# Moving the routing steps inside one attention turn of a fused encoder, attention and expert kernel

## The chip, the cores and the metric

One core of a Trainium2 chip runs the whole program in one launch. The metric is the device time of the launch in microseconds (us). Its engines are TensorE (PE in the rows, with its weight loads as PEld), VectorE (DVE), ScalarE (ACT), GpSimd (POOL) and SyncE, which issues most transfers (SPq). Each engine works through its own queue in order, and they meet at semaphores.

## The reference, cut to what matters

```python
h = concat([patch_tokens(x), text_encoder(x_txt)], axis=1)      # 8 batches, 49 + 512 = 561 rows, 192 columns
h = h + attention(layernorm(h))                                 # 12 heads of 64, diagonal masked out
h = h + experts(layernorm(h))                                   # 8 experts, the best 2 of each row

# attention
dots = einsum('bhid,bhjd->bhij', q, k) * scale[None, :, None, None]
dots = where(diag, MASK_VAL, dots)
out = einsum('bhij,bhjd->bhid', softmax(dots), v) @ W_out.T + b_out

# experts, of which the first part is "routing"
logits = x @ gate_w
top_w, top_i = top_k(softmax(logits), 2)
out = sum over the two experts of top_w * (gelu(x @ w_up + b_up) @ w_down + b_down)
```

## The kernel before

The program has three phases: the text encoder (the first 2,200 us or so), the attention with the routing of its result (to about 3,760 us), and the expert blocks. The change is in the second phase, `attention_phase`.

**Turns.** The attention handles one batch of 561 rows in a turn, in five row tiles of 128, 128, 128, 128 and 49. Twelve heads are taken in three groups of four. The turns are ten stretches of code, called regions: AHEAD (what a first turn finds already done), FIRST, SECOND, a hardware loop of five iterations, FINAL and CLOSE. SECOND, the loop's body and FINAL are made from the same hand-written order, the string `A_ORDER` (line 1006), in which each letter is the next step of one stream; FINAL leaves out what would belong to a further batch. CLOSE is not made from the string: it runs four output projections and then all routing steps in a row. FIRST has no routing. So the routing of batch n is in the turn of batch n+1, and seven turns out of eight hold it through the string.

**The steps** (`batch_steps`, line 1018) and what each engine does for one:

- `q`: `("t", c)` transposes the rows, `("qk", "q" or "k", h)` projects a pair of heads. TensorE multiplies (L1364), ScalarE rounds (L1475, L1477), VectorE takes the rest (L1717, L1720).
- `m`: `("max", h, i)` is TensorE's scores of head h, row tile i (L1392, with the mask L1395), then VectorE's row maximum (L1737). `s`: `("sum", h, i)` is ScalarE's exponential with its sum over the same PSUM buffer (L1453, an ACTIVATE and an ACTIVATION_READ_ACCUMULATOR).
- `s` also holds `("lse", g)`, ScalarE's logarithm (L1459) and VectorE's subtraction (L1703). `x`: `("maxt", g)` transposes the shift (L1401, L1483, L1725).
- `e`: `("exp", h, i)` is TensorE's transposed scores (L1392), ScalarE's exponential (L1489) and, for odd heads, GpSimd's clearing of the diagonal (L1292).
- `p`: `("pv", p, i)` is the product with the values (L1412), which waits for GpSimd, and `("take", p)` VectorE's copy of it (L1708). `v`, `w`: values (L1372, L1732) and output projection (L1421, L1743). `l`: the layer norm of the next batch (`("ln", 0)` L1506 and L1510, `("ln", 1)` L1515).
- `r`: the 80 steps of `ROUTE` (line 1009): `stats`, `rsqrt` (GpSimd), `norm` (L1543), ten pairs `mult` (L1549, 128x768) and `add` (L1553) for the logits, then 46 steps on arrays of 5 to 320 elements per partition, and ten `scatter` steps, each an indirect transfer issued by GpSimd (L1304). Among the small ones are `("r", "exp")` on ScalarE (L1463) and `("count",)`, which is a matmul: TensorE waits for `sel` (L1594), multiplies it with two constant matrices (L1427), and VectorE copies the result (L1746). Nearly every routing step waits for the one before it.

**PSUM buffers.** Every TensorE step of the kinds t, qk, v, max, maxt, exp, wo and count takes one of three ring buffers (`Region`, line 105, hands them out in the order in which the steps that end a use stand in the string). TensorE waits at the step until ScalarE or VectorE has finished the buffer's previous use; for a `max` that is the `sum` of the same head and tile. As it is in order, all that stands behind the step waits too.

The wait of the count step and what follows, in TensorE's queue and in VectorE's:

```python
elif kind == "count":
    pe.sem_inc(tick, 1)
    await_step(pe, R, it, "route", ("r", "sel"), now)
    ...
v.wait_ge(mm, R.done(it, "mm", step, now + 1))
    ...
elif kind == "count":
    nc.vector.tensor_copy(count[...], buf[:, :, 0:5 * E]).then_inc(dve, 1)
```

In the order before, the routing letters are spread almost evenly over the turn: `stats` is letter 33 of 327 (counted from 0), `norm` 51, the pairs 55 to 122, the small steps 126 to 294 with about two other steps between each two, `sel` 172, `count` 181, and the scatters 298 to 326. Six other TensorE steps stand between `sel` and `count`.

Of the kernel before, what the change touches and what calls it, by code (L numbers as in the profile page):

```python
# [1002 lines left out]

A_ORDER = "qqvweevewemsqvmvsmmsmssqevmwsmeswreereemmsmpsmsmsmsrspermmsrspreemrserqmprmsrpesrpmrsmsrqeerlsrpperqprxemresrmsprqpremsreerelermsmrqprmsermprsmsrsmrpsqrmersmprseeremremsrspremsmepseremrmpsrsqrmemrssmrsqrseprperqxqreprmmsrsmrspereemrsmrspereerpepremrmsmrsprsmsrmmsrmsreesrmsrmmsrpmrssermprseeremrepprsemrsmrseerserpeprperxpprprr"


ROUTE = ([("r", x) for x in ("stats", "rsqrt", "norm")] + [("r", x, j) for j in range(10) for x in ("mult", "add")]
# [8 lines left out]
def batch_steps(without=""):  # L1018
# [12 lines left out]
        "r": ROUTE}  # L1031
    assert sorted(A_ORDER) == sorted(k for k, v in streams.items() for _ in v)
    left = {k: iter(v) for k, v in streams.items()}
    steps = [(k, next(left[k])) for k in A_ORDER]
    ahead = lambda x: x[0] in ("t", "ln") or x in (("lse", 0), ("maxt", 0)) or (
# [1002 lines left out]
```

## Time and profile before

| | us |
|---|---|
| median of 3 runs | 4201.59 |
| lowest and highest | 4197.65, 4203.91 |
| profiled execution, its own time | 4201.37 |
| its span, first to last instruction | 4199.6 |
| busy: TensorE, VectorE, ScalarE, GpSimd | 3776.8, 2410.2, 2110.4, 1134.8 |
| mean granted TensorE clock, share of full | 0.947 |

The times are of the launch; the span leaves out some 1.8 us around it. Busy time is the union of an engine's instructions. An idle time in a row is the time just before the instruction in which its engine did nothing, followed by what ended it. The line number is that of the instruction in the code. Matmuls overlap a little, so that the times of two neighbours may add up to more than their distance.

### The profile page before, as it was taken

The numbers are of one execution on the slowest core, as the hardware profiler recorded it, in microseconds if no ns is written. First come the engines' busy times: TensorE is split into PE (matmuls) and PEld (weight loads), VectorE is DVE, ScalarE is ACT, GpSimd is POOL, SyncE is SP. The second block draws the span as 40 slices with busy tenths as digits, with TensorE's granted clock in tenths as the row PEclk, the third lists the DMA queues.
The fourth block names the chain that finished last, engine by engine and source line by source line (L and its number), as shares of the span: only waits on it lengthen the run. The fifth ranks groups of instructions, "written<-read, shape, count | busy, mean of one in ns | idle before, by whom it ended". The sixth has DMA issues, their size and how long they took to land. (4 is left out here: it accounts for less than half of the span.)

```text
span 4199.6 us, 64906 instructions
## 1 busy us (share of the span) xinstructions
PE 3776.8 (90%) x21662; PEld 2489.4 (59%) x21662; DVE 2410.2 (57%) x3929; ACT 2110.4 (50%) x3234; POOL 1134.8 (27%) x1036
## 2 busy tenths in 40 slices
PE   4899999999999999999984999999999999939998
PEld 3355555555555555555543676766666666628887
DVE  6566666666666666666642547566464655644443
ACT  0555545455554555545451666574665756613332
POOL 5132323223232333323222001111111121024444
PEclk7899999999999999999986999999999999969999
DMA  7242333423333233323335111111111111115564
GB/s 171 87 124 81 104 105 88 119 79 110 96 98 98 85 119 92 108 88 96 109 106 181 38 25 35 36 29 37 34 34 32 32 41 31 26 60 147 145 145 108
DMA packets 237689, 355.04 MB, mean 85 GB/s; under 512 B 40208, under 2 KB 138528, under 8 KB 234000
## 3 DMA queue, kind: packets, MB, share of 16 engines
q1 hardware_dynamic: 213344, 294.23, 24.3%
q0 software_dynamic: 23376, 57.40, 6.2%
q8 instruction: 118, 1.93, 0.2%
q10 hardware_dynamic: 768, 0.79, 0.1%
q14 instruction: 83, 0.68, 0.1%
HBM read 225.70 MB, written 112.63 MB: 81 GB/s over the span
## 5 line engine op out<-in xcount | busy, mean ns | idle before, releaser
L643 DVE TENSOR_REDUCE mx<-ring 128x2 f32<-128x1024 f32 x768 | 919.7, 1222 | 507.0 <-PE ring L406 503.3
L535 ACT ACTIVATE probs<-ring 128x1024 f32<-128x1024 f32 x768 | 767.2, 1024 | 416.6 <-PE ring L419 415.6
L1453 ACT ACTIVATE a_ring<-a_ring,a_nmx 128x561 f32<-128x561 f32 (+1 forms) x480 | 333.9, 696 | 239.5 <-DVE a_nmx L1737 238.0
L1737 DVE TENSOR_REDUCE a_nmx<-a_ring 128x1 f32<-128x561 f32 (+1 forms) x480 | 344.1, 735 | 191.5 <-PE a_ring L1392 96.2
L406 PE MATMUL ring<-k_stack,q_stack 48*128 48x512 f32 x1536 | 359.3, 480 | 63.9 <-ACT probs L535 23.3
L1292 POOL TENSOR_SCALAR_AFFINE_SELECT a_probs<-a_probs 128x256 f32<-128x256 f32 (+1 forms) x240 | 100.2, 418 | 1155.5 <-ACT a_probs L1489 1108.9
L419 PE MATMUL ring<-q_stack,k_stack 64*128 64x512 f32 x1536 | 362.9, 489 | 53.3 <-DVE mx L643 39.4
L433 PE MATMUL acc<-probs,vals 128*32 128x512 f32 x3072 | 399.7, 641 | 1.3 <-ACT probs L535 1.3
L1489 ACT ACTIVATE a_probs<-a_ring 128x561 f32<-128x561 f32 (+1 forms) x480 | 287.2, 636 | 179.0 <-PE a_ring L1392 175.9
L1392 PE MATMUL a_ring<-a_k_hh,a_q_hl 128*128 128x256 f32 (+1 forms) x960 | 312.4, 340 | 27.8 <-DVE a_q_hl L1717 12.7
L1392 PE MATMUL a_ring<-a_q_hl,a_k_hh 128*128 128x256 f32 (+1 forms) x960 | 289.7, 326 | 30.8 <-ACT a_ring L1453 21.5
L419 PEld LDWEIGHTS ring<-q_stack,k_stack 64*128 64x128 f32 x1536 | 142.8, 189 | 287.9 <-DVE mx L643 101.4
L406 PEld LDWEIGHTS ring<-k_stack,q_stack 48*128 48x128 f32 x1536 | 145.7, 192 | 280.2 <-DVE mx L643 83.0
L1412 PE MATMUL a_acc<-a_probs,a_vals 128*64 128x305 f32 (+1 forms) x1920 | 276.2, 413 | 7.4 <-POOL a_probs L1292 7.4
L479 PE MATMUL ring<-w,relu 128*128 128x192 f32 x1536 | 279.7, 332 | 1.4 <-ACT relu L542 1.4
L1392 PE MATMUL a_ring<-a_k_l,a_q_hm 128*128 128x256 f32 (+1 forms) x960 | 272.3, 292 | 0.0
L479 PEld LDWEIGHTS ring<-w,relu 128*128 128x128 f32 x1536 | 246.3, 190 | 33.6 <-issue 31.1
L1392 PE MATMUL a_ring<-a_q_hm,a_k_l 128*128 128x256 f32 (+1 forms) x960 | 264.6, 292 | 0.0
L49 POOL TENSOR_SCALAR var_eps<-mv 128x4 f32<-128x4 f32 (+1 forms) x65 | 14.9, 228 | 846.0 <-DVE mv L578 845.7
L1392 PEld LDWEIGHTS a_ring<-a_q_hl,a_k_hh 128*128 128x128 f32 (+1 forms) x960 | 168.1, 175 | 118.2 <-ACT a_ring L1453 45.4
L1364 PE MATMUL a_ring<-a_xT,a_wqk 96*128 96x256 f32 (+1 forms) x768 | 218.3, 433 | 16.6 <-issue 12.9
L1924 ACT ACTIVATE m_hid<-m_ring,m_table 128x512 f32<-128x512 f32 x150 | 103.0, 687 | 255.8 <-PE m_ring L1903 255.8
(231 smaller groups left out, 6949.7 us busy)
## 6 DMA issues: line engine op xcount, KB each, us to landing
q_stack<-qk_scratch SPq DMA_DIRECT2D x576, 64.0 KB, 2.4
k_stack<-qk_scratch SPq DMA_DIRECT2D x576, 64.0 KB, 2.4
qk_scratch<-qk_hi SPq DMA_DIRECT2D x32, 768.0 KB, 3.6
qk_scratch<-qk_lo SPq DMA_DIRECT2D x32, 768.0 KB, 5.2
a_q_hm<-a_q_hl SPq DMA_DIRECT2D x48, 280.5 KB
a_k_hh<-a_k_hh SPq DMA_DIRECT2D x48, 280.5 KB
tokens<-h_out SPq DMA_DIRECT2D x33, 384.0 KB, 2.7
h_in<-tokens SPq DMA_DIRECT2D x32, 384.0 KB, 4.1
```

Of the source, the lines that this page charges most:

```text
L406: last = nc.tensor.matmul(buf[:, r, :], q_st[s][terms, t, P * i:P * i + P], k_st[s][terms, t, :], start=True, stop=True)
L419: last = nc.tensor.matmul(buf[:, r, :], k_st[s][terms, t, P * kt:P * kt + P], q_st[s][terms, t, :], start=True, stop=True)
L433: last = nc.tensor.matmul(acc[g % 2][32 * hh:32 * hh + 32, :], vals[s][:, kt, 4 * (n // 2) + hh, :], probs[n % 2][:, hh, j, :], start=(n % ...
L479: last = nc.tensor.matmul(buf[:, i // 2, D * (i % 2):D * (i % 2) + D], relu[:, k2, P * i:P * i + P], w2[:, k2, :], start=(k2 == 0), stop=( ...
L535: nc.scalar.activation(probs[n % 2][:, pair:pair + 2, x // 2, :], buf[:, :, :], ACT.Exp, scale=DK ** -0.5).then_inc(act, 1)
L643: nc.vector.tensor_reduce(mx[s][:, i, :].rearrange("p (r t) -> p r t", r=2)[:, :, t], buf[:, :, :], AX, ALU.max).then_inc(dve, 1)
L1364: last = nc.tensor.matmul(flat(buf)[:, n0:n0 + n], wqk[:, c, P * j:P * j + P], xT[:, c, n0:n0 + n], start=(c == 0), stop=(c == 1))
L1392: last = nc.tensor.matmul(flat(buf)[0:r, n0:n0 + w], a, b[:, n0:n0 + w], start=(m == 0), stop=(m == 1 and not masked))
L1412: last = nc.tensor.matmul(flat(acc)[DH * r:DH * r + DH, n0:n0 + w], vals[:, i, 2 * p + r, :], probs[i][:, r, n0:n0 + w], start=(i == 0), s ...
L1453: nc.scalar.activation(buf, buf, ACT.Exp, bias=nmx[0:r, i, h:h + 1], accum_out=sums[0:r, i, h:h + 1]).then_inc(act, 1)
L1489: nc.scalar.activation(probs[i][0:r, h % 2, :], flat(buf)[0:r, 0:N], ACT.Exp).then_inc(act, 1)
L1737: nc.vector.tensor_reduce(nmx[0:r, i, h:h + 1], flat(buf)[0:r, 0:N], AX, ALU.max, negate=True).then_inc(dve, 1)
```

## The change

One string is replaced. The letters other than `r` stand in the same order as before; only the places of the 80 `r` among them differ. As the buffers are handed out by that order, the count step also takes its buffer at another place.

```diff
-A_ORDER = "qqvweevewemsqvmvsmmsmssqevmwsmeswreereemmsmpsmsmsmsrspermmsrspreemrserqmprmsrpesrpmrsmsrqeerlsrpperqprxemresrmsprqpremsreerelermsmrqprmsermprsmsrmsrpsqrmersmprseeremremsrspremsmepseremrmpsrsqrmemrssmrsqrseprperqxqreprmmsrsmrspereemrsmrspereerpepremrmsmrsprsmsrmmsrmsreesrmsrmmsrpmrssermprseeremrepprsemrsmrseerserpeprperxpprprr"
+A_ORDER = "qqvweevewemsqvmvsmmsmssqevmwsmeswreereemmsmpsmsmsmsrsrrpremmrrssperermserqmpmsprersprmsmsqeerlspperqpxermersmsprqpermsereerlemsmqpmsermpsrmssmprsqmerrsmprrrrserrrerrrerrrrmerrrrmssprrrrerrrmsmrerrrprrrrserrrerrrmrmprrrrssqmerrmssmrsqserprrrrprreqxqepmmssmspeeemsmspeeepepemmsmspsmsmmsmseesmsmmspmssempseeemeppsemsmseesepeppexppp"
```

Expanded, around the two places that the text below speaks of (route steps with their names, the others as step names):

```
before  norm, sum 6 2, pv 0 1, exp 2 0, mult 0, max 6 3, max 6 4, sum 6 3, add 0, sum 6 4, pv 0 2, mult 1, exp 3 0, exp 2 1
after   norm, sum 6 2, mult 0, add 0, pv 0 1, mult 1, exp 2 0, max 6 3, max 6 4, add 1, sum 6 3, sum 6 4, pv 0 2, exp 3 0, mult 2, exp 2 1

after   max 10 0, pv 2 2, total, inv, share, gt, sum 10 0, exp 5 3, eq, tie, over, exp 4 4, rank, mark, is_k, exp 5 4,
        sel, count, weight, run 0, max 10 1, exp 6 0, run 1, run 2, run 3, run 4, max 10 2, ...
```

After the change `stats`, `rsqrt` and `norm` are at the same letters. The pairs stand at 53 to 136, `top` at 142, `total` to `own4` at 152 to 217, `sel` at 166 with `count` right behind it at 167, and the scatters at 223 to 242. Behind letter 242 there is no routing.

## Rows read from the trace of the kernel before

**Rows 1.** The page: span and busy time of each engine.

```profile
span 4199.6 us, 64906 instructions
PE 3776.8 (90%) x21662; PEld 2489.4 (59%) x21662; DVE 2410.2 (57%) x3929; ACT 2110.4 (50%) x3234; POOL 1134.8 (27%) x1036
```

**Rows 2.** Windows, busy time by turn: SECOND and a loop turn.

```profile
core 0: us, PE busy (x) PEld busy (x) DVE busy (x) ACT busy (x) POOL busy (x), PEclk, DMA share, GB/s
2496.20:2667.40 171.20, 162.29 (x1007) 116.75 (x1005) 105.58 (x204) 108.67 (x219) 23.32 (x43) 1.00 0.14 33
...
2842.10:3020.10 178.00, 165.89 (x1006) 118.79 (x1006) 105.65 (x204) 108.85 (x219) 27.75 (x47) 0.98 0.14 34
```

**Rows 3.** Windows inside that loop turn, from its start at 2842.10.

```profile
2906.00:2937.00 31.00, 25.93 (x159) 17.83 (x159) 28.32 (x50) 20.70 (x40) 4.19 (x7) 1.00 0.18 43
2937.00:2959.00 22.00, 22.00 (x153) 16.40 (x153) 11.75 (x26) 16.20 (x36) 1.91 (x5) 1.00 0.08 21
```

**Rows 4.** Waits of TensorE in the same turn: total us, times, longest.

```profile
PE a_ring L1364 <- issue: 6.2, 2, 3.2
PE a_ring L1392 <- ACT a_ring L1453: 3.8, 6, 1.2
PE a_acc L1412 <- POOL a_probs L1292: 1.0, 1, 1.0
```

**Rows 5.** Timeline behind `norm`, the same turn: VectorE, ScalarE, TensorE.

```profile
2894.70 0.96 DVE L1549 TENSOR_TENSOR r_prod<-r_xw,r_gate 128x768 f32<-128x768 f32 x1
...
2895.57 1.37 DVE L1737 TENSOR_REDUCE a_nmx<-a_ring 128x1 f32<-128x561 f32 x2
2896.34 0.70 ACT L1453 ACTIVATE a_ring<-a_ring,a_nmx 128x561 f32<-128x561 f32 x1 [1.47 <-DVE a_nmx L1737]
...
2897.21 0.39 PE L1392 MATMUL a_ring<-a_q_hl,a_k_hh 128*128 128x256 f32 x1
```

**Rows 6.** Timeline at `max 10 0` and `exp 5 4`, the same turn.

```profile
2943.96 0.74 DVE L1737 TENSOR_REDUCE a_nmx<-a_ring 128x1 f32<-128x561 f32 x1 [0.22 <-PE a_ring L1392]
...
2946.47 0.30 PE L1392 MATMUL a_ring<-a_q_hm,a_k_l 128*49 128x306 f32 x1
```

**Rows 7.** Timeline of CLOSE, where the routing steps run alone, one behind the other.

```profile
3716.02 0.96 DVE L1549 TENSOR_TENSOR r_prod<-r_xw,r_gate 128x768 f32<-128x768 f32 x1
3717.01 0.95 DVE L1553 TENSOR_REDUCE r_logits<-r_prod 128x4 f32<-128x768 f32 x1
...
3736.55 0.20 DVE L1562 TENSOR_REDUCE r_total<-r_pr 128x5 f32<-128x40 f32 x1 [0.30 <-ACT r_pr L1463]
...
3740.32 0.20 DVE L1594 TENSOR_TENSOR r_sel<-r_is_k 128x40 f32<-128x40 f32 x1
3740.57 0.65 PE L1427 MATMUL a_ring<-r_sel,r_before 128*128 128x40 f32 x2 [30.74 <-DVE r_sel L1594]
...
3741.68 0.24 DVE L1746 COPY r_count<-a_ring 128x80 f32<-128x80 f32 x1 [1.17 <-PE a_ring L1427]
...
3747.99 0.19 DVE L1683 TENSOR_TENSOR r_owner<-r_owner,r_owner_add 128x25 f32<-128x25 f32 x1
```

**Rows 8.** `qk q 0`, `max 11 3`, the clearing of `exp 7 3`, `pv 3 3`; CLOSE's last transfer.

```profile
2959.09 1.62 DVE L1717 SCALAR_TENSOR_TENSOR a_q_hl<-a_ring,a_scales,a_q_hl 64x561 fp32r<-64x561 f32 x2 [1.07 <-ACT a_q_hl L1475]
...
2960.77 0.39 PE L1392 MATMUL a_ring<-a_k_hh,a_q_hl 128*128 128x256 f32 x1 [1.30 <-DVE a_q_hl L1717]
...
2970.40 0.41 POOL L1292 TENSOR_SCALAR_AFFINE_SELECT a_probs<-a_probs 128x256 f32<-128x256 f32 x1 [9.36 <-ACT a_probs L1489]
...
2976.48 1.17 PE L1412 MATMUL a_acc<-a_probs,a_vals 128*64 128x256 f32 x8
...
3758.71 0.95 POOL L1304 DMA_INDIRECT slots_in<-r_xw,r_slot  x1 [0.30 <-issue]
```

**Rows 9.** FINAL: a stall of TensorE, then the window with the granted clock.

```profile
3616.04 0.39 PE L1392 MATMUL a_ring<-a_q_hl,a_k_hh 128*128 128x256 f32 x1 [0.72 <-ACT a_ring L1453]
...
3616.80:3620.20 3.40, 3.40 (x17) 1.68 (x16) 2.36 (x5) 3.33 (x6) 1.18 (x1) 0.50 0.24 52
```

More of the change, by code:

```diff
@@ L993 @@
 PAIRS = H2 // 2
-A_ORDER = "qqvweevewemsqvmvsmmsmssqevmwsmeswreereemmsmpsmsmsmsrspermmsrspreemrserqmprmsrpesrpmrsmsrqeerlsrpperqprxemresrmsprqpremsreerelermsmrqprmsermprsmsrsmrpsqrmersmprseeremremsrspremsmepseremrmpsrsqrmemrssmrsqrseprperqxqreprmmsrsmrspereemrsmrspereerpepremrmsmrsprsmsrmmsrmsreesrmsrmmsrpmrssermprseeremrepprsemrsmrseerserpeprperxpprprr"
+A_ORDER = "qqvweevewemsqvmvsmmsmssqevmwsmeswreereemmsmpsmsmsmsrsrrpremmrssperermserqmpmsprersprmsmsqeerlspperqpxermersmsprqpermsereerlemsmqpmsermpsrmssmprsqmerrsmprrrrserrrerrrerrrrmerrrrmssprrrrerrrmsmrerrrprrrrserrrerrrmrmprrrrssqmerrmssmrsqserprrrrprreqxqepmmssmspeeemsmspeeepepemmsmspsmsmmsmseesmsmmspmssempseeemeppsemsmseesepeppexppp"
 ROUTE = ([("r", x) for x in ("stats", "rsqrt", "norm")] + [("r", x, j) for j in range(10) for x in ("mult", "add")]
```

## The prediction

> **What bounds the kernel now.** I read the page first: TensorE is busy for 90% of the span and VectorE for 57% [rows 1]. Only the attention's turns are touched, so next come the windows by turn: a turn lasts 171.2 us in SECOND, of which TensorE works 162.3, and 178.0 in the loop [rows 2]. TensorE sets the pace, and what a turn can gain or lose is TensorE's idle time. The waits tell where that is [rows 4]: 6.2 us of "issue" in two waits are the loop's branch at both ends of the window, which the change does not touch. The others in the turn come to 9 us: most end with ScalarE's exponential of a `sum`, which itself waited for VectorE's maximum, and 1.0 us ends with GpSimd.
>
> Windows inside the turn show a stretch where VectorE is the limit: from 2906 to 2937 it is busy for 28.3 of 31 us and TensorE for 25.9 [rows 3], so that 5.1 of the 9 us of idle time lie there. Right behind, from 2937 to 2959, TensorE has no idle time at all and VectorE works for 11.8 of 22 us [rows 3]. That is the room into which the change puts the small steps. But the room is a sum over 22 us; what counts is how long VectorE is away at a stretch, since three PSUM buffers let TensorE run only about two steps ahead.
>
> **Part 1, the pairs move up behind `norm`.** Before, VectorE does `mult 0` at 2894.70 and then the maxima of `max 6 3` and `max 6 4` from 2895.57; ScalarE's `sum 6 3` starts at 2896.34, and TensorE enters `exp 2 1`, which needs that buffer, at 2897.21, practically without waiting [rows 5]. So maximum to TensorE's start is 1.64 us. After, `add 0` and `mult 1` also stand in front. Alone, a `mult` or `add` takes 0.99 us start to start [rows 7], so the maxima start 1.98 us later, and so does `exp 2 1`: **+2.0 us**. Nothing covers it: the TensorE steps in between are the same, and TensorE's queue stands behind `exp 2 1`.
>
> What becomes of this in the stretch that VectorE limits? I followed both queues to `max 9 0` with the durations of these rows (0.65 us for a maximum start to start, 0.95 for a `mult` or `add`, and 0.87 from ScalarE's start to the free buffer). The delay is 3.1 us at `exp 3 2`, as two pairs now come before `max 7 3` where one and a half did; 1.4 at `exp 3 4`, since `mult 6` and `add 6` no longer stand before `maxt 1`; and 1.7 at `max 9 0`. VectorE has one pair (1.9 us) less to do by then, but gives most of it away waiting for ScalarE at `qk q 8`. So 0.3 comes back. Bounds for this part: 0 (the pair less is worth all of the 2.0) and 3.1 (nothing is made up). I take +1.7, the end of my chain.
>
> **Part 2, the small steps in a block, `count` right behind `sel`.** VectorE's maximum of `max 10 0` ends at 2944.70, TensorE has finished `exp 5 4` at 2946.77 [rows 6], and its next step is now `count`. Eleven VectorE steps from `total` to `sel` stand between. Run alone, they take from 3736.55 to 3740.52, 3.97 us, and TensorE's matmul follows 0.05 later [rows 7]. So TensorE waits until about 2948.75: **+2.0 us** (a delay from part 1 shifts both engines alike). Before, six steps of TensorE stood between `sel` and `count`, and no wait there is among the turn's [rows 4].
>
> The pages have a rule against my chain. In the rows a step that needs the one before starts 0.04 us after its end (3716.98 to 3717.01), while an independent maximum starts 0.09 before the end of the `mult` in front (2895.57 against 2895.66) [rows 5, 7], so a block of dependent steps costs more than the same steps spread out. The Trainium skill ("VectorE: DVE Perf Modes", section "The DRAIN you can't avoid") has it that the semaphore between VectorE operations costs nothing extra. By that rule the block would be some 0.13 x 10 = 1.3 us shorter and this stall 0.7 us; the rows differ, and I go by them.
>
> From the copy of `count` (3741.68) to `own4` (end 3748.18) the rest takes 6.5 us alone [rows 7]. In the turn six maxima and a `take` at 0.65 lie between, so VectorE reaches `qk q 0` about 11 us after the copy at 2949.9, at 2960.9 instead of 2959.09 [rows 8]. `max 11 3`, which waits for it (1.30 us of idle time before, until 2960.77 [rows 8]), starts about 2.0 later than before: the count's delay arrives whole. Behind it VectorE has no routing, and the 0.5 us wait at `qk k 0` goes. Part 2: +1.5; bounds 0.7 (the rule's stall) and 2.5.
>
> **Part 3, the last third.** The scatters leave the turn's end, where GpSimd's clearing for `pv 5 4` stood behind them: the 1.0 us wait on GpSimd goes [rows 4]. At their new place ten of them hold GpSimd for 10 x (0.95 + 0.30) = 12.5 us [rows 8] between the clearings of `exp 7 2` and `exp 7 3`, where it was idle for 9.36, so the second, at 2970.40, comes some 3 us later. Its reader `pv 3 3` starts at 2976.48 [rows 8], so I cost that at nothing; if the transfers take longer beside other work, up to 1.5. VectorE's lighter end of turn gains nothing: TensorE does not wait for it there. SyncE's queue holds no routing step, and its load at `take 0` waits for `norm`, which stays. Part 3: -1.0, bounds -1.5 and +0.5.
>
> **The sum.** 1.7 + 1.5 - 1.0 = +2.2 us a turn, in seven turns +15.4. Granted clock: in FINAL it fell to half for 3.4 us right behind a stall of 0.72 us [rows 9], although the loop turn keeps the full clock in the same stretch [rows 3]. Such a drop costs at most 1.7. I take one in half of the turns at 1.2: +4. On the profile's own 4201.4 (its median is 4201.6, the same) that is **4220 us**.
>
> **The rivals.**
> - *Delay absorbed.* Part 1 is made up entirely and part 2 leaves 0.7 to 1: with the scatters' -1.0 a turn changes by -0.5 to +0.5, the whole by some 4 us, **4201**. For it: 5.1 us of idle time in the stretch of [rows 3] could shrink. Against: it follows the stall, and VectorE is full there.
> - *Faster.* If VectorE, not the ring, sets the end of that stretch, the pair less is worth 1.9 us at `max 9 0`, TensorE comes to `count` no earlier than `sel`, and GpSimd's 1.0 and the 0.5 at `qk k 0` go: -3.4 a turn, **4177**. It decides if TensorE's idle time up to `max 9 0` falls below the present 6 us. Against it is `exp 2 1`, where the order alone gives +2.0.
> - *The clock falls with each new stall.* A loop turn is 6.8 us longer than SECOND's [rows 2]; 3.1 of that is the branch's idle time, so the half clock behind it costs some 3.5. One such stretch a turn at the `count` or `exp 2 1` stall adds 24: **4241**; two, 4266. For it: the new stalls of 2 us lie between those of up to 1.3, mostly without a drop, and the branch's 3.2, with one. The Trainium skill ("TensorE: Matmul & The Clock Gate", section "Part 1: The HAM clock gate") says that half rate is the default and only recent activity lifts it, which speaks for this rival.
> - That the order does other than it says can't be: the other letters are unchanged.
>
> **How the numbers follow.** A measurement of this kernel tells 0.2% (8.4 us) from no change. Forecast 0.52 (4208 to 4232), absorbed 0.22 (4195 to 4209), faster 0.13, clock 0.13 (4232 to 4266). The range that leaves out the faster case and the top of the clock's is 4199 to 4242. Faster by over 0.2% (below 4193): 0.13; within (to 4210): 0.26; slower: 0.61, the rest of the forecast and all of the clock case.
>
> **What would show it.** TensorE's waits should have a new one at L1427 on `sel`, some 2 us in each of seven turns, and one of about 2 at `exp 2 1`; the wait on GpSimd at the turn's end should be gone; SECOND should last about 173.5 us, and the waits in a turn sum to 11 instead of 9. The forecast is wrong if L1427 waits under 1 us (the block is faster or covered), if SECOND stays at 171 (absorbed), or if windows around the stalls show half clock (last rival).

## The result, and the profile after

The changed kernel takes **4277.2 us** (median of 4 runs, 4275.1 to 4282.5); the kernel before takes 4199.6 beside it (4 runs). The ratio is 1.0186, 95% interval 1.0174 to 1.0198, so 78 us slower. Forecast were 19. The direction was right, the size was four times too small and outside the range.

The page of the changed kernel:

```profile
span 4274.6 us, 64906 instructions
PE 3808.3 (89%) x21662; PEld 2510.7 (59%) x21662; DVE 2418.0 (57%) x3929; ACT 2109.6 (49%) x3234; POOL 1132.9 (27%) x1036
```

Against [rows 1] VectorE, ScalarE and GpSimd do the same work; TensorE is busy for 31.5 us more with the same instructions, and idle for 43.5 us more. The windows by turn tell where: SECOND, a loop turn, and the sum over the seven turns.

```profile
2496.05:2677.26 181.21, 167.51 (x1008) 119.84 (x1006) 107.22 (x204) 108.67 (x219) 27.43 (x47) 0.96 0.14 33
2863.63:3050.00 186.37, 167.33 (x1006) 119.56 (x1006) 107.32 (x204) 108.66 (x219) 27.39 (x46) 0.96 0.13 32
...
sum 1278.05, PE 1157.06 PEld 826.88 DVE 727.32 ACT 735.92 POOL 191.16; mean PE 165.29 PEld 118.13 DVE 103.90 ACT 105.13 POOL 27.31
```

The same sum for the kernel before:

```profile
sum 1203.46, PE 1127.65 PEld 806.47 DVE 719.27 ACT 737.00 POOL 190.85; mean PE 161.09 PEld 115.21 DVE 102.75 ACT 105.29 POOL 27.27
```

So the seven turns are 74.6 us longer, 45.2 of it TensorE's idle time (121.0 instead of 75.8) and 29.4 longer busy time for the same matmuls: the mean granted clock of a loop turn is 0.94 to 0.96 instead of 0.98 to 1.00. SECOND lasts 181.2 us (171.2 in [rows 2]), where the prediction said 173.5. Now TensorE's waits in the loop turn of the row above, which answers to [rows 4]:

```profile
PE a_ring L1364 <- ACT a_probs L1489: 6.5, 1, 6.5
PE a_ring L1364 <- issue: 5.8, 2, 3.0
PE a_ring L1392 <- ACT a_ring L1453: 5.1, 6, 2.0
PE a_ring L1427 <- DVE r_sel L1594: 1.9, 1, 1.9
```

Two of the predicted signs are there: 1.9 us at L1427 on `sel`, and a longest wait of 2.0 at L1392, which is `exp 2 1`. The wait on GpSimd at the turn's end is gone. But the first row was not predicted at all: 6.5 us at L1364, at the step `qk k 2`. The five loop turns have 6.3 to 6.6 us there, SECOND has 2.1, FINAL, which has no such step, none. The timeline shows the two predicted stalls as the prediction had them ([rows 5], [rows 6]):

```profile
2915.73 1.37 DVE L1737 TENSOR_REDUCE a_nmx<-a_ring 128x1 f32<-128x561 f32 x2
2916.49 0.70 ACT L1453 ACTIVATE a_ring<-a_ring,a_nmx 128x561 f32<-128x561 f32 x1 [3.46 <-DVE a_nmx L1737]
...
2917.36 0.39 PE L1392 MATMUL a_ring<-a_q_hl,a_k_hh 128*128 128x256 f32 x1 [2.03 <-ACT a_ring L1453]
...
2966.75 0.20 DVE L1594 TENSOR_TENSOR r_sel<-r_is_k 128x40 f32<-128x40 f32 x1
2967.01 0.42 PE L1427 MATMUL a_ring<-r_sel,r_before 128*128 128x40 f32 x2 [1.94 <-DVE r_sel L1594]
```

From the maximum's start to TensorE's it is 1.63 us, as before. The third stall looks like this, first on GpSimd, then on ScalarE and TensorE:

```profile
2983.49 1.10 POOL L1304 DMA_INDIRECT slots_in<-r_xw,r_slot  x1 [0.46 <-issue]
...
2991.23 0.96 POOL L1304 DMA_INDIRECT slots_in<-r_xw,r_slot  x1 [0.30 <-issue]
...
2995.02 0.95 POOL L1304 DMA_INDIRECT slots_in<-r_xw,r_slot  x1 [0.30 <-issue]
2998.96 0.40 POOL L1292 TENSOR_SCALAR_AFFINE_SELECT a_probs<-a_probs 128x256 f32<-128x256 f32 x1 [2.99 <-ACT a_probs L1489]
...
2990.73 0.64 ACT L1489 ACTIVATE a_probs<-a_ring 128x561 f32<-128x561 f32 x1
2998.15 0.64 ACT L1489 ACTIVATE a_probs<-a_ring 128x561 f32<-128x561 f32 x1 [6.78 <-remote]
...
2998.84 4.11 PE L1364 MATMUL a_ring<-a_xT,a_wqk 96*128 96x256 f32 x8 [6.46 <-ACT a_probs L1489]
```

ScalarE's `exp 6 3` ends at 2991.37 and `exp 7 3` starts only at 2998.15. By the code it waits for nothing but TensorE's count of finished steps, and TensorE's matmuls for it were over by about 2990. From 2983.49 to 2995.97 GpSimd issues its ten scatters, 1.27 us apart.

The trace also keeps the time at which each step's semaphore event arrives. In this turn five TensorE steps end 4.7, 5.6, 6.3, 8.2 and 8.9 us behind the start of the first scatter; the third of them is `exp 7 3`. Their events are recorded at 7.5, 13.9, 14.6, 14.7 and 14.8 us. In the kernel before each of TensorE's events is recorded within 0.03 us of the step's end. So ScalarE starts late because TensorE's event comes 8.3 us late. And behind the stalls the clock is at its lower level (1.2 GHz): the windows behind `count` and around `qk k 2` have PEclk 0.50.

```profile
2967.90:2971.30 3.40, 3.40 (x17) 2.88 (x17) 2.19 (x9) 1.35 (x3) 0.00 (x0) 0.50 0.00 0
2995.20:3005.40 10.20, 6.56 (x20) 4.11 (x20) 3.82 (x5) 4.50 (x7) 1.17 (x2) 0.50 0.18 39
```

### The profile page after: what moved, and what is told of

It reads as the page before. It is cut to its first block and busy times, and to the rows that moved or that the text cites. A ratio compares the mean times of both kernels' runs of the same rounds, so it can differ in the third digit from the quotient of the medians.

```text
span 4274.6 us, 64906 instructions
## 1 busy us (share of the span) xinstructions
PE 3808.3 (89%) x21662; PEld 2510.7 (59%) x21662; DVE 2418.0 (57%) x3929; ACT 2109.6 (49%) x3234; POOL 1132.9 (27%) x1036
## 5 line engine op out<-in xcount | busy, mean ns | idle before, releaser
L1392 PE MATMUL a_ring<-a_k_hh,a_q_hl 128*128 128x256 f32 (+1 forms) x960 | 315.6, 343 | 25.7 <-DVE a_q_hl L1717 11.5
L1392 PE MATMUL a_ring<-a_q_hl,a_k_hh 128*128 128x256 f32 (+1 forms) x960 | 295.6, 332 | 35.2 <-ACT a_ring L1453 31.6
L1392 PE MATMUL a_ring<-a_k_l,a_q_hm 128*128 128x256 f32 (+1 forms) x960 | 275.1, 295 | 0.0
L1364 PE MATMUL a_ring<-a_xT,a_wqk 96*128 96x256 f32 (+1 forms) x768 | 231.3, 453 | 47.9 <-ACT a_probs L1489 34.7
L1392 PE MATMUL a_ring<-a_q_hm,a_k_l 128*128 128x256 f32 (+1 forms) x960 | 269.2, 296 | 0.0
L1392 PEld LDWEIGHTS a_ring<-a_q_hl,a_k_hh 128*128 128x128 f32 (+1 forms) x960 | 171.4, 179 | 122.2 <-ACT a_ring L1453 54.6
L49 POOL TENSOR_SCALAR var_eps<-mv 128x4 f32<-128x4 f32 (+1 forms) x65 | 14.8, 228 | 846.4 <-DVE mv L578 846.1
```

Of the source, the lines that this page charges most:

```text
L1364: last = nc.tensor.matmul(flat(buf)[:, n0:n0 + n], wqk[:, c, P * j:P * j + P], xT[:, c, n0:n0 + n], start=(c == 0), stop=(c == 1))
L1392: last = nc.tensor.matmul(flat(buf)[0:r, n0:n0 + w], a, b[:, n0:n0 + w], start=(m == 0), stop=(m == 1 and not masked))
```

## The experiments

Most change only the order, and are written by the places of the steps: a place is the number of other letters (of 247) ahead of the step. In the kernel before the scatters stand at 228, 231, 233, 236, 238, 241, 243, 246, 247, 247, in the changed one at 153, 153, 157, 161, 162, 162, 162, 162, 163, 163. `qk k 2` is place 166. The table has for each the median (of 4 to 10 runs), the ratio to the kernel before, and of the profiled run the sums over the seven turns, read as above. Idle time in it includes the branch's wait of some 2.8 us between turns, which the expectations leave out where they speak of 9.5 or 16 us a turn.

| kernel | us | ratio (95%) | TensorE idle | busy |
|---|---|---|---|---|
| before | 4199.6 | | 75.8 | 1127.7 |
| changed | 4277.2 | 1.0186 (1.0174-1.0198) | 121.0 | 1157.1 |
| scatters back | 4227.6 | 1.0067 (1.0051-1.0084) | 87.9 | 1141.7 |
| scatters singly | 4218.4 | 1.0043 (1.0030-1.0055) | 78.3 | 1142.8 |
| block of ten at 192 | 4275.7 | 1.0180 (1.0163-1.0197) | 126.2 | 1152.0 |
| scatters back, `count` apart | 4210.5 | 1.0025 (1.0015-1.0035) | 76.4 | 1137.1 |
| scatters back, pairs back | 4213.3 | 1.0035 (1.0022-1.0049) | 86.0 | 1133.0 |
| five and five | 4224.8 | 1.0062 (1.0046-1.0078) | 82.5 | 1148.0 |
| seven and three | 4227.1 | 1.0070 (1.0055-1.0085) | 84.9 | 1145.4 |
| ten, 192 to 215 | 4227.1 | 1.0071 (1.0055-1.0086) | 83.8 | 1144.5 |
| before, block of ten at 243 | 4207.8 | 1.0019 (1.0010-1.0029) | 78.0 | 1134.1 |
| seven, clearing, three | 4222.7 | 1.0058 (1.0035-1.0080) | 80.2 | 1145.8 |
| eight, clearing, two | 4256.6 | 1.0139 (1.0122-1.0156) | 101.2 | 1161.7 |
| nine, clearing, one | 4261.0 | 1.0150 (1.0129-1.0172) | 106.5 | 1153.8 |
| ten, short pause inside | 4261.6 | 1.0155 (1.0138-1.0172) | 114.5 | 1146.8 |
| ten, one wait inside | 4227.8 | 1.0066 (1.0050-1.0083) | 83.3 | 1146.8 |
| version 1 | 4180.6 | 0.9955 (0.9938-0.9972) | 60.1 | 1124.4 |
| version 2 | 4171.5 | 0.9935 (0.9922-0.9949) | 54.8 | 1118.1 |

**Where do the 78 us come from?** First the scatters alone were moved, in three ways.

```
-scatters 153 153 157 161 162 162 162 162 163 163
+scatters back:   228 231 233 236 238 241 243 246 247 247
+singly:          153 163 173 183 193 203 213 223 233 243
+block of ten:    192 192 192 192 192 192 192 192 192 192
```

> The changed kernel with only the ten scatters put back to their places of before (the turn's end, one every two or three steps). The changed kernel takes 4277.2. Theory 'block' (the ten scatters back to back are what stalls `qk k 2` for 6.5 us and drops the clock behind it): that stall is gone in all seven turns, the 1.0 us wait on GpSimd at `pv 5 4` comes back, TensorE's idle time in a loop turn falls from 16 to about 10.5 us, and the time is 4277 - 5 x 8.5 - 10 + 7 = about 4232 (4222 to 4240). Rival 'small stalls' (the 2.0 us waits at `exp 2 1` and at `count`, with the half clock behind each, are what costs): the stall at `qk k 2` may go, but the half-clock stretches stay and TensorE's tail only shifts; the time stays at 4255 or above.

> The changed kernel with the scatters one by one, at every tenth step from where its block begins to the turn's end (153, 163, ... 243 of 247). 'Block': no stall at `qk k 2` and no wait on GpSimd at `pv 5 4`, so 7 us below the kernel with the scatters back at the end: about 4225 (4215 to 4235). Rival 'place' (any scatter beside SyncE's copies of the q and k heads holds TensorE's events back): two of the ten still fall there, so a stall of 1 to 3 us stays at `qk k 2`, 4235 to 4250. 'Small stalls': 4255 or above.

> The changed kernel with the ten scatters still in one block, but at step 192 of 247, some 20 us later in the turn, where SyncE issues no copies of q or k heads. 'Block': the late TensorE events and a stall of 4 us or more appear at the new place instead of `qk k 2`, and the time stays at 4262 or above. Rival 'copies' (the scatters only hurt beside SyncE's 280.5 KB copies): no stall over 2 us at the new place and 4220 to 4235. 'Small stalls': 4255 or above in either case, with the half clock still behind `exp 2 1` and `count`.

The times of the theory "block" were met in all three: 4227.6 (4232 expected), 4218.4 (4225), and 4275.7 with the block elsewhere (4262 or above), where no copy of q or k heads is issued. Its one stall of 4 us or more did not come there in the loop turn that I read: TensorE's idle time is 6.6 us more than with single scatters, but in several waits, the longest 3.6. In one turn VectorE, too, starts a maximum 4.3 us late ("<-remote"), so the late events are not ScalarE's own trouble. So the block costs 59 us (4277.2 to 4218.4), and with single scatters the changed kernel is 19 us slower than before, which happens to be the forecast. Neither is SyncE's traffic needed nor that place in the turn.

**Parts 1 and 2**, on the kernel with the scatters back.

```
-count 130, weight 130 ... own4 148 (behind sel at 130)
+count 143, weight 143 ... own4 161      (count apart)
-mult 0 50, add 0 50, mult 1 51 ... add 9 114
+mult 0 52, add 0 55, mult 1 57 ... add 9 100      (pairs back)
```

> The kernel with the scatters back (4227.6) and, besides, `count` and all small steps behind it 13 steps later, so that 13 steps stand between `sel` (130) and `count` (143). It undoes the stall of part 2. Theory 'idle time only' (my prediction's part 2: the stall costs 1.5 us a turn net and the clock hardly anything): 7 x 1.5 = 10.5 less, 4217. Theory 'idle and clock' (in five of seven turns the granted clock of that kernel is half for 3.4 us right behind the `count` stall, and each such stretch costs 1.2 to 1.7 us): the half-clock stretches at `max 10 1` / `max 10 2` go too, and the time falls by 10.5 + 5 x 1.5 = 18 to about 4210 (4206 to 4213).

> The kernel with the scatters back (4227.6) and, besides, the ten pairs at their places of before (52 to 100); the small steps stay in their block. It undoes part 1. My prediction's part 1 has +1.7 us of idle time a turn: 4227.6 - 12 = 4216. Rival read from the trace of the changed kernel (the waits of 0.72 at `exp 2 3`, 0.93 at `exp 3 4` and 0.26 at `max 8 0` come back when the 2.03 at `exp 2 1` goes, so that hardly any idle time is saved; what part 1 costs is the half clock behind `exp 2 1`): idle time of a turn about the same (10.3 to 10.6), the half-clock stretch at `exp 2 1` / `exp 3 1` gone, time 4227.6 - 5 x 1.5 = about 4220 (4216 to 4223).

`count` apart: 17.1 us less, as "idle and clock" had it; 11.5 of the turns' sum is idle time, 4.6 busy time. Pairs back: 14.3 us less by the medians, 10.5 by the turns' sums, so about 4 us of the difference between the medians are not seen in the turns. Idle time falls by 1.9 us in all seven turns together where the prediction had 12, busy time by 8.7. So the reading of the rival was right, though the time lies below its range of 4216 to 4223. The waits of a loop turn without part 1 show what stands in the place of the 2.0 us:

```profile
PE a_ring L1392 <- ACT a_ring L1453: 3.7, 6, 1.2
PE a_ring L1364 <- issue: 3.0, 1, 3.0
PE a_ring L1427 <- DVE r_sel L1594: 1.9, 1, 1.9
PE a_ring L1392 <- DVE a_q_hl L1717: 1.9, 2, 1.3
PE a_acc L1412 <- POOL a_probs L1292: 1.0, 1, 1.0
PE a_ring L1392 <- DVE a_xT L1725: 0.9, 1, 0.9
```

With part 1 (scatters back):

```profile
PE a_ring L1392 <- ACT a_ring L1453: 4.7, 5, 2.0
...
PE a_ring L1427 <- DVE r_sel L1594: 1.9, 1, 1.9
PE a_ring L1392 <- DVE a_q_hl L1717: 1.6, 2, 1.3
```

The 2.0 us at `exp 2 1` replace 0.9 on `a_xT` at `exp 3 4`, 0.7 at `exp 2 3` and 0.3 at `max 8 0`: further down VectorE makes up almost all of the delay.

**How long may the block be?** At places without SyncE's copies:

```
-192 x10
+five and five:    192 x5, 220 x5
+seven and three:  192 x7, 220 x3
+ten, 192 to 215:  192 195 197 200 202 205 207 210 212 215
```

> The changed kernel with the block of ten scatters cut in two of five, at step 192 and at step 220 of 247 (the whole block at 192 took 4275.7, single scatters 4218.4). 'Length of the block' (TensorE's events come late only from about the fifth scatter on, as the first four in a row do no harm in the kernel before): no stall over 1 us at either place, 4218 to 4226. Rival 'every scatter that follows another directly costs its share': half-sized stalls at both places, sum as before, 4262 to 4278. Between them 4235 to 4255 would say that the backlog grows with the square of the length.

> The changed kernel with its scatters in a block of seven at step 192 and one of three at step 220 (ten at 192 took 4275.7; five and five 4224.8, with 9.5 us of idle time in a loop turn, as with single scatters, 9.5). Theory 'threshold' (what is in flight or queued drains while up to five or six are issued, and each one beyond holds TensorE's events back by some 1.3 to 1.6 us): idle time of a loop turn 9.5 + 2 x 1.4 = 11 to 12.5, time 4235 to 4248. Rival 'only long blocks' (seven are still harmless, the backlog needs the full ten): 9.5 us and 4215 to 4228. Rival 'all beyond five': as bad as ten, 15 to 16 us and 4262 or above.

> The changed kernel with its ten scatters from step 192 to 215, one every two or three steps (192, 195, 197, 200, ...), so some 1.5 to 2 us apart instead of 1.27. Theory 'rate' (the scatters' packets and their semaphore events queue up faster than they are served only when they follow directly): no late TensorE events, idle time of a loop turn 9.5 to 9.8, 4216 to 4226. Rival 'number within some 15 us': a stall of 2 us or more at steps 205 to 215, idle time 12 or more, 4240 or above.

Five and seven are harmless in the loop turns: a turn has 12 us of idle time with the branch's, as with single scatters, and 19 with ten. What they cost over single scatters lies in FINAL, where the clearing of `exp 9 3` stands behind scatters and `pv 4 3` waits 3.8 (five) and 6.4 us (seven) for it. My "threshold" of five or six with a graded cost from there on was wrong. The run with places 192 to 215 was meant to spread them but did so hardly: in its trace GpSimd issues six directly, then the clearing, then four, the tenth 12.3 us behind the first instead of 11.5. Yet it is free of the stall, at 4227.1, one microsecond above the range of its theory. So the stall goes although the ten are hardly further apart in time.

The same block of ten was put into the kernel before, at its end:

```
-228 231 233 236 238 241 243 246 247 247
+243 x10
```

> The kernel before with one thing changed: its ten scatters stand in one block at step 243 of 247, behind the clearing of `exp 11 4`. The 1.0 us wait on GpSimd at `pv 5 4` goes in any case (-7). 'Block': from the fifth scatter on TensorE's events come late, now at the seam and in the next turn's first steps; a stall of 4 to 6 us a turn appears there with the half clock behind it, 4199.6 - 7 + 7 x 8 = about 4248 (4235 to 4260). Rival 'place' (at the seam TensorE has slack, its steps there read no fresh buffer): 4193 to 4205.

8 us slower, between the two: the 1.0 us at `pv 5 4` goes, and at the start of three turns TensorE waits 2.1 to 4.9 us at `v 1`; in the others 0.5 at most. This is another stall than the one at `qk k 2`. It runs through data: `v 1` needs the buffer of `wo 0`, VectorE empties that only when GpSimd has added the output bias to the token rows (L1280), and this addition stands behind the ten scatters:

```profile
2677.55 0.94 POOL L1304 DMA_INDIRECT slots_in<-r_xw,r_slot  x1 [0.30 <-ACT a_probs L1489]
2678.52 2.34 POOL L1280 TENSOR_TENSOR a_tok<-a_tok,a_bout 128x768 f32<-128x768 f32 x2
...
2680.90 0.36 DVE L1743 TENSOR_TENSOR a_tok<-a_ring,a_tok 128x192 f32<-128x192 f32 x1 [6.46 <-POOL a_tok L1280]
...
2681.31 4.95 PE L1372 MATMUL a_ring<-a_wv,a_xT 96*128 96x384 f32 x8 [4.89 <-DVE a_tok L1743]
```

How long the wait is follows from how early TensorE comes there: where `v 0` starts 4.7 us behind the first scatter the wait is 4.9, at 7.5 it is 2.1, at 9.1 or more 0.5 at most. And TensorE's events are on time in all these turns, within 0.03 us, although the ten scatters follow each other directly, 11.5 us from the first to the tenth as in the changed kernel. So a row of ten does not make events late by itself. What else it needs is open.

**Place, clearing, or queue?** Now at the change's own place, with the last few scatters behind GpSimd's clearing of `exp 7 3`:

```
-153 153 157 161 162 162 162 162 163 163
+seven, clearing, three:  153 153 157 161 162 162 162   164 164 164
+eight, clearing, two:    153 153 157 161 162 162 162 162   164 164
+nine, clearing, one:     153 153 157 161 162 162 162 162 163   164
```

> The changed kernel with its last three scatters moved from steps 162 and 163 to step 164, that is behind GpSimd's clearing of `exp 7 3`; nothing else differs, and the ten stand where the change put them. Seven now follow each other directly and three come behind the clearing. 'Length of the block' (ten in a row hold TensorE's events back, seven with a gap behind them don't, whatever lies beside them): the stall of 6.5 us at `qk k 2` is gone from the loop turns, their idle time is 9.5 to 10 us instead of 16, the 5.4 us wait in the last turn is 2 to 4, and the time 4217 to 4230. Rival 'place' (beside SyncE's q and k copies a shorter block suffices): the stall stays at 3 us or more, 4245 or above.

> The changed kernel with its last two scatters (instead of three) behind GpSimd's clearing of `exp 7 3`: eight in a row, the clearing, two. With three behind it took 4222.7, with none 4277.2. 'Unbroken row' with its limit at or above eight: idle time of a loop turn 9.5 to 10, 4220 to 4232. With the limit between seven and eight: a stall of 1 us or more at `qk k 2`, 4235 or above. 'Late clearing': the clearing is then some 1.3 us later than in that kernel; a graded stall of 1 to 3 us, 4235 to 4250.

> The same with only the last scatter behind the clearing: nine in a row, the clearing, one. 'Unbroken row' with its limit at nine or ten: 9.5 to 10 us of idle time a loop turn and 4222 to 4234. Limit below: a stall of 3 us or more, 4250 or above. 'Late clearing': a graded stall of 3 to 5 us, 4250 to 4262.

Seven: no stall at `qk k 2` in any turn. Eight: 3.4 to 3.5 us in the loop turns, nine: 3.1 to 4.8, ten: 6.3 to 6.6. The step is between seven and eight. Nine alone would not tell "limit below" from "late clearing", whose range also holds 4261.0; eight does, with 4256.6 above the latter's 4235 to 4250. With seven, ScalarE's two exponentials follow each other (the scatters start at 2970.22):

```profile
2977.97 0.96 POOL L1304 DMA_INDIRECT slots_in<-r_xw,r_slot  x1 [0.30 <-issue]
2978.93 0.42 POOL L1292 TENSOR_SCALAR_AFFINE_SELECT a_probs<-a_probs 128x256 f32<-128x256 f32 x1
...
2977.46 1.17 ACT L1489 ACTIVATE a_probs<-a_ring 128x561 f32<-128x561 f32 x2
```

With eight (the first starts at 2975.99):

```profile
2985.01 0.96 POOL L1304 DMA_INDIRECT slots_in<-r_xw,r_slot  x1 [0.30 <-issue]
2988.43 0.40 POOL L1292 TENSOR_SCALAR_AFFINE_SELECT a_probs<-a_probs 128x256 f32<-128x256 f32 x1 [2.46 <-ACT a_probs L1489]
...
2983.24 0.64 ACT L1489 ACTIVATE a_probs<-a_ring 128x561 f32<-128x561 f32 x1
2987.62 0.64 ACT L1489 ACTIVATE a_probs<-a_ring 128x561 f32<-128x561 f32 x1 [3.74 <-remote]
```

`exp 7 3` could have started at 2983.88, but the eighth scatter starts at 2985.01. ScalarE is held up **before** the eighth scatter runs. The events tell the same. With eight, the five TensorE steps end 4.7, 5.6, 6.4, 8.3 and 8.9 us behind the first scatter and their events come at 7.3, 10.2, 11.6, 11.7 and 11.8; with seven the steps end at the same distances and the events come within 0.03 us. Until then the two kernels have run the same scatters, so what differs is the instruction that stands behind the seventh in GpSimd's queue, not a transfer that has run. And the clearing is late because ScalarE is late, not the other way round. Two kernels test that with the order untouched:

```diff
 g.indirect_dma_start(slots_in, ...).then_inc(scattered, 16)
+if (i, k) == (3, 0):                       # pause inside
+    for n in range(4): nc.gpsimd.memset(pause[:, n, :], 0.0)
```

> The changed kernel, order untouched, with four small memsets of a tile that nothing reads on GpSimd behind the seventh scatter (0.1 us each by the rows of such memsets in the kernel before), so that the row of ten is broken by some 0.45 us while the clearing of `exp 7 3` still stands behind all ten and is as late as before. Theory 'unbroken row' (ten scatters in direct succession hold TensorE's events back; any break restores them): stall at `qk k 2` gone, idle time of a loop turn about 9.5 to 10 us, time 4218 to 4232 (the last turn keeps its wait of 5 us for the clearing). Rival 'late clearing' (what matters is that GpSimd's clearing stands behind the scatters and comes late): the stall stays at 6 us or more, 4270 or above.

```diff
+if (i, k) == (3, 1):                       # wait inside
+    await_step(g, R, it, "act", ("exp", 6, 3), now)
+    g.sem_inc(tick, 1)
 g.indirect_dma_start(slots_in, ...).then_inc(scattered, 16)
```

> The changed kernel, order untouched, with one wait more on GpSimd: before its eighth scatter it waits for ScalarE's `exp 6 3` (in the changed kernel that ends 7.9 us after the first scatter's start, the eighth starts at 9.0, so the wait costs GpSimd next to nothing), and the clearing of `exp 7 3` still stands behind all ten. In the run with eight in a row ScalarE's `exp 7 3` was already late at 7.8 us after the first scatter, before the eighth had started by the record; so what hurts may be how many scatters GpSimd's queue holds in a row without a wait. Theory 'a wait in the row' : the stall of 6.5 us goes, idle time of a loop turn 9.5 to 10 us, 4220 to 4234. Rival 'clearing behind all ten' or 'the ten's density in time': stall of 4 us or more, 4255 or above.

The memsets only put the eighth scatter 0.11 us later (1.38 us behind the seventh instead of 1.27), and stalls of 4.5 to 5.5 us stay: neither rival had that number, and "any break restores them" is wrong. The wait takes the stall away altogether: 49 us for one semaphore wait (with the counter step that the program puts behind it) that is met 1.1 us before the eighth scatter starts. Its trace (lines are 3 higher):

```profile
2972.91 1.10 POOL L1307 DMA_INDIRECT slots_in<-r_xw,r_slot  x1 [0.46 <-issue]
...
2980.65 0.96 POOL L1307 DMA_INDIRECT slots_in<-r_xw,r_slot  x1 [0.30 <-issue]
2981.91 0.96 POOL L1307 DMA_INDIRECT slots_in<-r_xw,r_slot  x1 [0.30 <-ACT a_q_hl L1478]
...
2984.44 0.95 POOL L1307 DMA_INDIRECT slots_in<-r_xw,r_slot  x1 [0.30 <-issue]
2985.40 0.42 POOL L1292 TENSOR_SCALAR_AFFINE_SELECT a_probs<-a_probs 128x256 f32<-128x256 f32 x1
...
2980.15 1.17 ACT L1492 ACTIVATE a_probs<-a_ring 128x561 f32<-128x561 f32 x2
```

Tenth scatter 11.53 us behind the first, as in the changed kernel: the same ten transfers at the same pace, the clearing still behind them, and ScalarE runs both exponentials in a row. TensorE's events come within 0.03 us again. What differs is how many scatters GpSimd can take up without a wait. Whether the counter step alone would do, or a wait at another place in the row, was not tried.

**Versions meant to beat both.**

```
 version 1: pairs evenly 52 to 118; top ... sel 121 to 146; count 150; weight ... own4 152 to 222;
            scatters 226 228 230 232 234 236 243 244 246 247
 version 2: pairs 52 56 59 62 65 68 74 79 90 94 102, then nine steps 106 to 128;
            top ... sel 130 to 147; count 151; weight ... own4 153 to 222; scatters as in version 1
```

> A version meant to beat both: the ten pairs evenly from step 52 to 118 (before: 52 to 100), the small steps singly from 121 to 146, `count` at 150, four steps behind `sel` (146), the rest singly to 222, and the scatters at 226, 228, 230, 232, 234, 236, then 243, 244, 246, 247, so that none stands ahead of the clearing of `exp 11 4` (242). If VectorE is what makes TensorE wait in the stretch from `max 7 3` to `max 9 0`, one pair in seven steps instead of one in five takes 1 to 3 us off its idle time, and 1.0 at `pv 5 4` goes: 7 x 2 to 4 us below before, 4172 to 4190. Rival (the waits are set by the ring's order of steps and hardly by the pairs): 4190 to 4200, of which the 7 us at `pv 5 4`.

> The version that took 4180.6 with its pairs thinned out where TensorE waits for VectorE's stretch: three pairs from step 52 to 68, then 74, 79, 90, 94 and 102, nine steps from 106 to 128, small steps to 147, `count` at 151 (four behind `sel`), the rest to 222, scatters unchanged. If the pairs set the waits at `exp 2 3` (0.72), `max 8 0` (0.53) and `max 9 0` (0.68), they shrink by 1 us a turn together: 4172 to 4178. Rival (they are set by ScalarE's and the ring's order): unchanged, 4178 to 4184; a new wait at steps 110 to 130, where VectorE then has nine more of its 0.95 us steps, would put it above 4184.

Version 1: 4180.6, within its range. Version 2: **4171.5**, 28 us below the kernel before, and 0.5 below the range that its better theory gave. In its loop turn TensorE's waits are

```profile
PE a_ring L1364 <- issue: 5.5, 2, 2.8
PE a_ring L1392 <- ACT a_ring L1453: 3.0, 6, 1.2
PE a_ring L1392 <- DVE a_q_hl L1717: 1.7, 2, 1.4
PE a_ring L1392 <- ACT a_probs L1489: 0.5, 2, 0.3
```

No stall at `exp 2 1`, none at `count`, no wait on GpSimd: by the traces both versions have at most five scatters in direct succession, and only the first six of the ten stand ahead of the clearing of `exp 11 4`.

## Why the prediction was right and wrong

- **Part 1, the stall.** Predicted +2.0 at `exp 2 1`, measured 2.03. Right, by the same rows.
- **Part 1, what becomes of it.** Predicted +1.7 us of idle time a turn; shown were 0.3 (1.9 in seven turns). The chain through the stretch that VectorE limits came out too long: the waits at `exp 2 3` and `exp 3 4` went and the one at `max 8 0` halved, which the prediction knew only as a lump of 5.1 us [rows 3]. The rival "absorbed" was right in this. Yet the part costs 10.5 us by the turns' sums and 14 by the medians, 8.7 of it longer busy time, that is the clock.
- **Part 2.** Predicted 2.0 at `count` and 1.5 net; measured 1.94 and 11.5 / 7 = 1.6. Right, but for the clock behind the stall, 4.6 us of busy time in the seven turns. The row of dependent steps cost what CLOSE's rows [rows 7] said; by the rule of the Trainium skill ("VectorE: DVE Perf Modes", section "The DRAIN you can't avoid") it would have been 0.7, and the trace does not agree with that. (The pair of rows that the prediction quotes gives 0.03 us from end to start of a dependent step, not 0.04; nothing hangs on it.)
- **Part 3, the turn's end.** Predicted -1.0 for the wait on GpSimd; it went.
- **Part 3, the new place: the step that failed.** "Its reader `pv 3 3` starts at 2976.48 [rows 8], so I cost that at nothing", with +0.5 as the upper bound. Measured: 49 us in all for the row of ten (changed kernel against the one with a wait inside), 6 to 10 us in each of six turns, stall and clock together. I had looked for who reads the late clearing, and so for the one path that goes through data. The stall took another one: with ten scatters behind each other TensorE's events came up to 8.3 us late. In FINAL that path through data does exist as well: with fewer steps between, `pv 3 3` waits 5.4 us for the clearing. I had costed one turn's rows for all seven.
- **The clock.** Predicted +4, one drop in half of the turns. In the kernel with the scatters back, whose two stalls are all that is new, the trace has a half-clock stretch of 3.4 us right behind `exp 2 1` in five turns and right behind `count` in five; busy time is 14.0 us longer. The price of a drop (1.4, if all of it is put down to these ten; 1.2 predicted) was right, their number was three times too low. The last rival had the place right (a drop behind each new stall of 2 us) but charged 3.5 each. The trace agrees with what the prediction cited for that rival from the Trainium skill ("TensorE: Matmul & The Clock Gate", section "Part 1: The HAM clock gate"), that half rate is the default and only recent activity lifts it: ten of the fourteen new stalls have such a drop right behind them.
- **The other rivals.** "Faster" needed TensorE's idle time up to `max 9 0` to fall; it did not, `exp 2 1` alone added 2.0.
- **The sum.** Parts 1 and 2 without the block are +28 (scatters back), against 22 forecast for them and 4 for the clock: near, with two errors of opposite sign. Single scatters give +19, the same as the forecast by these two errors. Of the remaining 59 the row without a wait is 49, and most of the other 10 is FINAL's wait for the clearing (its turn lasts 156.9 us with the wait inside, 151.1 with single scatters).

## To carry to other kernels

Before instructions that start transfers are gathered into one block, count how many an engine can take up without waiting for anything; here seven were free in the loop turns and eight cost 3.4 us of TensorE a turn, and one wait ahead of the eighth restored 49 of 78 us. It does not hurt everywhere (ten in a row at the turn's end left all events on time), so test the place. And ask what else stands behind the block in that engine's queue: there it was the bias addition, which stopped TensorE for up to 4.9 us. A stall of 2 us costs more than its length once the clock falls behind it, so a delay that is made up later is not free. And price a step at its new place in each region that runs it, the shorter last turn too.

## What the hardware showed that I had not expected

- With eight or more indirect transfers in direct succession on GpSimd, in the middle of the turn, TensorE's completion events came late, by up to 8.3 us (`exp 7 3` waits "6.78 <-remote"), although nothing in the program joins the two. The delay begins before the eighth starts, is longer with more of them (3.4, up to 4.8, 6.5 us of stall for eight, nine and ten), and is gone if GpSimd has a semaphore wait in front of the eighth. Ten in direct succession at the end of the turn, in the kernel before, delayed no event by more than 0.03 us. So more than seven in a row was needed in these runs, but was not enough.
- The Trainium skill ("Advanced Engine Details and Errata", section "Engine Queue Depths") gives GpSimd a queue of 8. The limit between seven and eight in these runs is near it, but no trace here shows how full the queue was. How the block holds back another engine's events is not shown; the runs show only that the same ten transfers at the same pace do no harm with a wait among them, that SyncE's copies are not needed, and that a clearing behind all ten is not enough.
- A granted clock of 0.50 for 3.4 us followed the stalls of 1.9 to 2.0 us in most turns. Behind those of 1.2 to 1.4 in the same turns (`exp 5 1`, `max 11 3`) it was seldom, and only at `max 11 3` (in two turns each of the kernels with the pairs back and with `count` apart).
